# Attention and mixture-of-experts layer on one core: normalizations moved to ScalarE, both halves of the cross projections made by GpSimd

## What is computed

```python
x = layernorm(x + self_attention(x))            # 16 heads of 16, rotary q and k, no bias
x = layernorm(x + cross_attention(x, context))  # q from x; k, v from the context; biases b_q, b_k, b_v, b_o
x = layernorm(x + moe(x))                       # 8 experts, 2 chosen, 2 shared

def layernorm(x):                               # over the 256 features, no gain and no shift
    return (x - mean(x)) / sqrt(var(x) + 1e-5)
# cross attention: qh = q @ w_q.T + b_q, kh = k @ w_k.T + b_k, softmax(qh kh^T / 4) vh, then w_o, b_o
```

## Time and profile before

| | before |
|---|---|
| median of 3 runs | 1545.46 us |
| lowest and highest run | 1537.97 and 1546.08 us |
| the profiled execution, its own time | 1557.11 us |
| its span, first to last instruction | 1555.4 us |
| TensorE busy | 1402.5 us, 90% |
| VectorE busy | 1115.6 us, 72% |
| ScalarE busy | 907.3 us, 58% |
| GpSimd busy | 439.5 us, 28% |
| mean granted TensorE clock | 0.94 of full |

### The profile page before, as it was taken

The page is one execution under the profiler, slowest core; times in us unless marked ns, Lnnn a source line. Parts: engine busy times, 40 slices in busy tenths (PEclk is TensorE's granted clock), DMA queues, the critical chain, the costliest instruction groups (busy, mean ns, idle before and its releaser), DMA issues. The chain is left out here.

```text
span 1555.4 us, 27690 instructions
## 1 busy us (share of the span) xinstructions
PE 1402.5 (90%) x8424; PEld 845.7 (54%) x8424; DVE 1115.6 (72%) x2282; ACT 907.3 (58%) x1702; POOL 439.5 (28%) x411
## 2 busy tenths in 40 slices
PE   2889899999999999999999998999588889999984
PEld 2424354544435444454444443443277779999974
DVE  3788388888789888889879878757256544555466
ACT  3276547656666666666766676646245445555544
POOL 4211131032014013105103201100125544666654
PEclk8699889989999999999999999979789889999997
DMA  3451622433343343244243334140135435778762
GB/s 124 126 159 35 188 81 77 138 103 120 105 136 121 102 128 125 67 148 121 77 139 109 117 101 137 42 110 2 37 136 185 155 105 109 154 131 165 150 178 82
DMA packets 108089, 179.85 MB, mean 116 GB/s; under 512 B 20288, under 2 KB 65984, under 8 KB 103872
## 3 DMA queue, kind: packets, MB, share of 16 engines
q1 hardware_dynamic: 93376, 159.11, 33.1%
q0 software_dynamic: 14592, 19.41, 7.1%
HBM read 98.09 MB, written 79.30 MB: 114 GB/s over the span
## 5 line engine op out<-in xcount | busy, mean ns | idle before, releaser
L618 DVE TENSOR_REDUCE nm<-ps_max 128x1 f32<-128x512 f32 x1024 | 640.6, 681 | 107.0 <-PE ps_max L810 106.7
L576 ACT ACTIVATE prob<-ps_sc 128x512 f32<-128x512 f32 x1024 | 557.9, 597 | 267.5 <-PE ps_sc L824 262.9
L810 PE MATMUL ps_max<-qk 48*128 48x512 f32 x1024 | 442.2, 494 | 31.4 <-DVE nm L618 17.1
L824 PE MATMUL ps_sc<-qk 50*128 50x512 f32 x1024 | 406.6, 466 | 34.0 <-ACT prob L576 33.7
L824 PEld LDWEIGHTS ps_sc<-qk 50*128 50x128 f32 x1024 | 166.5, 189 | 346.5 <-ACT prob L576 294.4
L841 PE MATMUL ps_out<-prob,va 128*32 128x512 f32 x2048 | 279.7, 619 | 1.4 <-ACT prob L576 1.2
L810 PEld LDWEIGHTS ps_max<-qk 48*128 48x128 f32 x1024 | 177.6, 192 | 90.7 <-DVE nm L618 68.7
L1573 PE MATMUL ps_gu<-x2f,we 128*128 128x256 f32 (+1 forms) x1344 | 222.1, 320 | 4.6 <-ACT sg L1238 2.4
L1573 PEld LDWEIGHTS ps_gu<-x2f,we 128*128 128x128 f32 x1344 | 189.2, 191 | 21.9 <-DVE h L1464 3.1
L458 POOL TENSOR_TENSOR rstd<-mv,eps 128x2 f32<-128x2 f32 x32 | 6.4, 201 | 621.7 <-DVE mv L687 621.7
L1573 PE MATMUL ps_dn<-we,hf 128*128 128x256 f32 x864 | 122.6, 298 | 11.3 <-DVE totals L1547 10.5
(11 more groups left out here) (145 smaller groups left out, 1467.3 us busy)
## 6 DMA issues: line engine op xcount, KB each, us to landing
qk<-hbm_self SPq DMA_DIRECT2D x384, 64.0 KB, 2.4
qk<-hbm_cross SPq DMA_DIRECT2D x384, 64.0 KB, 2.3
hbm_self<-stage SPq DMA_DIRECT2D x16, 1024.0 KB, 4.0
hbm_cross<-stage SPq DMA_DIRECT2D x16, 1024.0 KB, 4.2
slots_x<-zeros SPq DMA_DIRECT2D x8, 1360.0 KB, 5.9
xs<-slots_x SPq DMA_DIRECT2D x40, 272.0 KB
weraw<-w_moe SPq DMA_DIRECT2D x11, 768.0 KB
x2in<-x SPq DMA_DIRECT2D x16, 512.0 KB, 4.3
```

Source lines behind the costliest of these rows:

```text
L576: nc.scalar.activation(prob[:, s % 2, j, :], ps_sc[:, (HG * s + j) % NSC, :], ACT.Exp, scale=HD ** -0.5).then_inc(exp_done[a], 1)
L618: nc.vector.tensor_reduce(nm[:, g % 2, r:r + 1], ps_max[:, n % NMX, :], axis=AX.X, op=ALU.max, negate=True).then_inc(max_done[a], 1)
L810: nc.tensor.matmul(ps_max[:, n % NMX, :], qk[rows, 0, pair, P * c:P * c + P], qk[rows, 1, pair, :], start=True, stop=True).then_inc(smax_d ...
L824: nc.tensor.matmul(ps_sc[:, n % NSC, :], qk[rows, 1, h // 2, P * c:P * c + P], qk[rows, 0, h // 2, :], start=True, stop=True).then_inc(st_ ...
```

## The change

The normalizations `ln0` and `ln1` move from VectorE to ScalarE, as an affine step: scale `rstd` and bias `shift` = -mean x `rstd`. GpSimd makes `shift`, by two more small instructions for each `w0` and `w1` half.

For `ck` and `cq`, ScalarE evicts the projection with its bias once, unrounded, into a new buffer `raw_ck` or `raw_cq`, and frees the bank of `ps_job` by that. GpSimd makes both halves from the buffer: the high part by adding a broadcast zero with an fp32r output, then the low part by subtraction. VectorE has no part in either any more. The wait for `self_out` moves from ScalarE to GpSimd, and SyncE's transfers to `hbm_cross` wait for GpSimd's `parts_done` instead of VectorE's count.

```diff
--- before.py
+++ after.py
@@ -90,7 +90,8 @@
 ORDER = [task for half in (FIRST, SECOND) for s in sorted(TASKS[half]) for task in TASKS[half][s]
          if task[0] in PER and task[0] not in ("x", "c")]
 assert len(ORDER) % 2 == 0
-SPLIT = ("q", "k", "ck", "cq", "xt", "nt0", "nt1", "nm0", "nm1", "x", "c")
+SPLIT = ("q", "k", "xt", "nt0", "nt1", "nm0", "nm1", "x", "c")
+KEPT_RAW = ("ck", "cq")
 
 
 def exists(b):
@@ -220,6 +221,9 @@
         res = sb("res", [P, TT, D])
         rot = res[:, :, :].rearrange("p (a u) d -> p a (u d)", a=2)
         cosq = sb("cosq", [P, 2, T])
+        job_raw = {kind: sb(f"raw_{kind}", [P, FC, T]) for kind in ("ck", "cq")}
+        shift = sb("shift1", [P, TT, 1])
+        mone = sb("mone1", [P, TT, 1])
         stage = sb("stage", [P, FC, SLOTS, T], F32R)
         qk = sb("qk", [P, 2, H // 2, T], F32R)
         va = sb("va", [P, 2, TT, H, 2 * HD])
@@ -254,6 +258,7 @@
         read = {k: sem(f"{k}_read") for k in job_done}
         hi_done = {k: sem(f"{k}_hi") for k in SPLIT}
         lo_done = {k: sem(f"{k}_lo") if k in ("q", "k", "x", "c") else read[k] for k in SPLIT}
+        parts_done = {k: sem(f"{k}_parts") for k in KEPT_RAW}
         sin_done = {k: sem(f"{k}_sin") for k in ("q", "k")}
         roped = {k: sem(f"{k}_roped") for k in ("q", "k")}
         self_out = [sem(f"self_out{m}") for m in range(FC)]
@@ -375,14 +380,14 @@
 
                 if h.name == "second" and isinstance(h.k, int) and h.k == -1:
 
-                    sp.wait_ge(consts, 6)
+                    sp.wait_ge(consts, 7)
                     sp.wait_ge(w_hi, 1)
                     sp.wait_ge(w_ready, 1)
                 for s in range(h.steps):
                     if s in h.cross and exists(h.cross[s][0]):
                         b, m = h.cross[s]
-                        sp.wait_ge(lo_done["cq"], upto("cq", b, m))
-                        sp.wait_ge(lo_done["ck"], upto("ck", b, m))
+                        sp.wait_ge(parts_done["cq"], 2 * upto("cq", b, m))
+                        sp.wait_ge(parts_done["ck"], 2 * upto("ck", b, m))
                         sp.dma_start(hbm_cross[m], stage[:, m, :, :].bitcast(F32)).then_inc(cross_out[m], 16)
                     for kind, n, b in h.table.get(s, []):
                         if kind in ("nm0", "nm1"):
@@ -424,17 +429,31 @@
             nc.gpsimd.memset(eps[:, :, :], EPS).then_inc(consts, 1)
             nc.gpsimd.memset(one[:, :], 1.0).then_inc(consts, 1)
             nc.gpsimd.memset(zeros[:, :], 0.0).then_inc(consts, 1)
-            pool.wait_ge(consts, 6)
+            nc.gpsimd.memset(mone[:, :, :], -1.0).then_inc(consts, 1)
+            pool.wait_ge(consts, 7)
             pool.wait_ge(consts_dma, 48)
 
             def split_lo(kind, b, n, out, value, high):
 
                 pool.wait_ge(hi_done[kind], upto(kind, b, n))
                 nc.gpsimd.tensor_tensor(out, value, high.bitcast(F32), ALU.subtract).then_inc(lo_done[kind], 1)
+
+            def both_parts(kind, b, n):
+
+                c = 2 if kind == "ck" else 0
+                pool.wait_ge(self_out[n], (b + 1 if exists(b + 1) else b) * 16 + 16)
+                pool.wait_ge(read[kind], upto(kind, b, n))
+                nc.gpsimd.tensor_tensor(stage[:, n, c + HI, :], job_raw[kind][:, n, :], zeros[:, 0:1].to_broadcast([P, T]), ALU.add) \
+                    .then_inc(parts_done[kind], 1)
+                pool.wait_ge(parts_done[kind], 2 * (b * 2 + n) + 1)
+                nc.gpsimd.tensor_tensor(stage[:, n, c + LO, :], job_raw[kind][:, n, :], stage[:, n, c + HI, :].bitcast(F32),
+                                        ALU.subtract).then_inc(parts_done[kind], 1)
 
             def half(h):
                 for s in range(h.steps):
                     for kind, n, b in h.table.get(s, []):
+                        if kind in KEPT_RAW:
+                            both_parts(kind, b, n)
                         if kind in ("q", "k"):
 
                             c = 0 if kind == "q" else 1
@@ -457,8 +476,13 @@
                             pool.wait_ge(mv_done[a], b * TT + 2 * n + 2)
                             nc.gpsimd.tensor_tensor(rstd[:, at, :], mv[:, at, 1:2], eps[:, at, :], ALU.add) \
                                 .then_inc(var_done[a], 1)
-                            pool.wait_ge(var_done[a], upto(kind, b, n))
+                            nc.gpsimd.tensor_tensor(shift[:, at, :], mv[:, at, 0:1], mone[:, at, :], ALU.mult) \
+                                .then_inc(var_done[a], 1)
+                            pool.wait_ge(var_done[a], 3 * (b * 2 + n) + 1)
                             nc.gpsimd.tensor_tensor(rstd[:, at, :], rstd[:, at, :], mhalf[:, at, :], ALU.pow) \
+                                .then_inc(var_done[a], 1)
+                            pool.wait_ge(var_done[a], 3 * (b * 2 + n) + 3)
+                            nc.gpsimd.tensor_tensor(shift[:, at, :], shift[:, at, :], rstd[:, at, :], ALU.mult) \
                                 .then_inc(rstd_done[a], 1)
                         if kind == "x1b":
                             pool.wait_ge(ln_done[SELF], b * TT + TT)
@@ -525,13 +549,23 @@
                     act.wait_ge(in_sem["c"], b * 16 + 16)
                     wait_done(act, job_done["w0"], "w0", b, 1)
                     split_hi("c", b, 0, cf[:, HI, :, :], raw[:, :, :])
-                if kind == "ck":
-
-                    act.wait_ge(self_out[n], (b + 1 if exists(b + 1) else b) * 16 + 16)
-                    split_hi(kind, b, n, stage[:, n, 2, :], bank(kind, n, b), bcol[:, 1, n:n + 1])
-                if kind == "cq":
-                    act.wait_ge(self_out[n], (b + 1 if exists(b + 1) else b) * 16 + 16)
-                    split_hi(kind, b, n, stage[:, n, 0, :], bank(kind, n, b), bcol[:, 0, n:n + 1])
+                if kind in KEPT_RAW:
+                    act.wait_ge(job_done[kind], upto(kind, b, n))
+                    if exists(b - 1):
+                        act.wait_ge(parts_done[kind], 2 * upto(kind, b - 1, n))
+                    c = 1 if kind == "ck" else 0
+                    nc.scalar.activation(job_raw[kind][:, n, :], bank(kind, n, b), ACT.Identity, bias=bcol[:, c, n:n + 1]) \
+                        .then_inc(read[kind], 1)
+                if kind in ("ln0", "ln1"):
+                    a = int(kind[2])
+                    if a == SELF:
+                        wait_done(act, job_done["xt"], "xt", b - 1, 1)
+                        if exists(b - 1):
+                            act.wait_ge(x1b_done, (b - 1) * TT + TT)
+                    for t in range(TT):
+                        act.wait_ge(rstd_done[a], b * 2 + t // 2 + 1)
+                        nc.scalar.activation((res if a else x1)[:, t, :], res[:, t, :], ACT.Identity,
+                                             scale=rstd[:, t, :], bias=shift[:, t, :]).then_inc(ln_done[a], 1)
                 if kind == "nt1":
                     wait_done(act, job_done["cv"], "cv", b + 1, 1)
                     split_hi(kind, b, n, nf[:, HI, n, :], bank(kind, n, b), bcol[:, 2, n:n + 1])
@@ -634,10 +668,6 @@
                     nc.vector.tensor_tensor(cosq[:, c, :], bank(kind, n, b), trig[:, 0, :], ALU.mult)
                     nc.vector.stream_shuffle(rot[:, c, :], bank(kind, n, b), [p ^ 1 for p in range(32)]) \
                         .then_inc(read[kind], 1)
-                if kind == "ck":
-                    split_lo(kind, b, n, stage[:, n, 3, :], stage[:, n, 2, :], bcol[:, 1, n:n + 1])
-                if kind == "cq":
-                    split_lo(kind, b, n, stage[:, n, 1, :], stage[:, n, 0, :], bcol[:, 0, n:n + 1])
                 if kind == "nt0":
                     split_lo(kind, b, n, nf[:, LO, n, :], nf[:, HI, n, :])
                 if kind == "nt1":
@@ -685,16 +715,6 @@
                     for t in (2 * n, 2 * n + 1):
                         wait_alone(dve, stat_done[a], b * TT + t + 1, w_hi, 1)
                         nc.vector.bn_aggr(mv[:, t, :], st6[:, t, :]).then_inc(mv_done[a], 1)
-                if kind in ("ln0", "ln1"):
-                    a = int(kind[2])
-                    if a == SELF:
-                        wait_done(dve, job_done["xt"], "xt", b - 1, 1)
-                        if exists(b - 1):
-                            dve.wait_ge(x1b_done, (b - 1) * TT + TT)
-                    for t in range(TT):
-                        dve.wait_ge(rstd_done[a], b * 2 + t // 2 + 1)
-                        nc.vector.tensor_scalar((res if a else x1)[:, t, :], res[:, t, :], mv[:, t, 0:1],
-                                                rstd[:, t, :], ALU.subtract, ALU.mult).then_inc(ln_done[a], 1)
 
             def half(h):
                 for s in range(h.steps):
...
```

More of the change, by code:

```diff
@@ L718, in _ @@
             pe.wait_ge(w_ready, 2)
-            pe.wait_ge(consts, 6)
+            pe.wait_ge(consts, 7)
             pe.wait_ge(w_hi, 1)
```

## The result

| | before | after |
|---|---|---|
| median of runs on one chip | 1544.05 us (4 runs, 1537.97 to 1546.08) | 1561.05 us (4 runs, 1556.41 to 1564.41) |
| ratio | | 1.0104, interval 1.0074 to 1.0134 |
| profiled execution | 1557.11 us | 1556.41 us |
| its span, its mean granted clock | 1555.4 us, 0.936 | 1554.7 us, 0.930 |

What follows compares the result with a forecast made beforehand. Bound by the scores-Exp ring, TensorE in projection steps, VectorE only in lumps. 7.4 + 1.9 - 6.0 + 3.8 - 0.8 + 1.4 + 0.75 = +8.5 us on 1545.5 gave 1554.0 us, range 1541 to 1563.

Steps and rivals of the forecast that it cites:

- the likeliest case: Whole kernel: lengthened and shortened steps sum to +8.5 us, 0.55% slower; chance 0.50, of which 0.35 above the bound.
- a rival with 0.13: Behind both closes' stalls: one more low-clock window of 12 us each, +7.2, so +15.7 in all, 1561 us; chance 0.13.
- The case's own range: Whole kernel: the forecast's own range around +8.5 us, +1 to +14.
- ln0 in the passes: Steps around ln0: ScalarE's four normalizations delay Exp, lateness handed on whole, +1.24 us a pass, six times: +7.4 us.
- The walk: Steps 11 to 13 around ln0: third score 1.17 us late, fourth 1.37, next Exp pair 1.25.
- ln1 in the passes: Step of ln1: wait for Exp replaces wait for a maximum, +0.1 us in five passes, +1.4 in the sixth: +1.9.
- ck and cq: Cross projections in the passes: VectorE's relief brings late maxima forward, -1.0 us a pass, six times: -6.0 us.
- The closes: Both closes: cross transfers leave 1.9 us later, +3.8 us; ln0 there ends 0.4 earlier each, -0.8 us.
- The rival that hides them: Closes: late cross projections are hidden there too, +4.7 us in all, 1550 us; chance 0.15.
- The end: ln1 of batch 6 on ScalarE +1.4 us; batch 7 in series, small instructions and last two tiles, +0.75 us.
- my own mark: Loop pass: 126.3 us becomes 126.6; forecast wrong if the pass shrank by a microsecond or more.

Runs made afterwards that it cites:

- cross_passes: Kernel before with only the cross projections of batches 1 to 6 on ScalarE and GpSimd, normalizations on VectorE: 1544.86 us, ratio 1.0000.
- ln_only: Kernel before with only the normalizations moved to ScalarE, cross projections as before: 1564.20 us, ratio 1.0148.
- cross_warm: cross_passes with the third maximum matmul of step 13 of each first half repeated five times: 1553.55 us, ratio 0.9917.
- before_warm: Kernel before with a maximum matmul of step 13 of each first half repeated five times: 1556.46 us, ratio 0.9963.
- before_x1b: Kernel before with only GpSimd's x1b held back until VectorE has done ln1: 1556.08 us, ratio 0.9951.
- cross_only: Kernel before with all cross projections by ScalarE and GpSimd, normalizations on VectorE: 1550.88 us, ratio 1.0042.
- after_again: The changed kernel, unchanged, run again against the kernel before on another chip: 1578.36 us, ratio 1.0105.
- the filling: One maximum matmul issued six times instead of once ahead of the wait behind ln1; changed kernel 1.0040, cross_passes so filled 0.9917, kernel before 0.9963.

## Why the prediction came out as it did, point by point

The direction was right and the time lay in the range. The size was off by a factor of two, and the sum behind it was not what cost the time: the likeliest case gave +8.5 us by its steps, of which some 2 were there; the rest was the clock, which I had as a rival with 0.13. The case's own range, +1 to +14 us, missed the 17; that 1561.05 us lies within 1541 to 1563 is owed to the room left for that rival, and to luck.

**ln0 in the passes, +7.4.** The mechanism was right: TensorE waits for Exp, and the lateness is handed on. The size was 0.75 + 0.17 = 0.92 us a pass, so +5.5. The walk had the third and fourth score 1.17 and 1.37 us late; in the pass shown, against that of the earlier trace rows, they were 0.93 and 1.08. It took the lateness as handed on whole, but the job behind the fourth maximum had stood 0.72 us behind the fourth score and now stands 0.51, and `ln0`'s own step ended only 0.75 us late. The step behind it added the 0.17.

**ln1 in the passes, +1.9.** One wait took the other's place, as forecast. The step became 0.19 us shorter instead of 0.1 longer, and the sixth pass 1.1 us longer for 1.4: together +0.15.

**ck and cq, -6.0.** I read four steps and had -1.0 a pass. The four steps gave -0.86; but the step at the loop's edge gave 0.52 more, four times, which I had not looked at, and the two such steps at the ends of the loop went from 4.46 to 4.23 and from 4.51 to 4.13. In all -7.8. `cross_passes` has -5.9 at equal clock. GpSimd's pair is hidden in the passes, as forecast.

**The closes, +3.8 and -0.8.** The transfer leaves 1.8 us later, for 1.9. What reaches the first maximum is 2.0 us in the first close (21.40 us from the eviction, for 19.36) and 1.2 in the second (14.78 for 13.60), where less of the delay reached it: +3.2. The rival that hides them is refuted. The steps of `ln0` in the closes fell from 5.04 to 4.13 and from 5.02 to 4.27 us, 0.8 each for the forecast 0.4: -1.65.

**The end, +1.4 and +0.75.** The lump of batch 6 costs 1.74 us: `cross_passes`, with the low clock there but VectorE's `ln1`, has 11.67 us for the three steps, and after 13.41. That is the most it can be, as the clock is low in the whole first of these steps in after and only at its end in `cross_passes`; `ln_only`, low for its last microsecond, has 13.11, which gives 1.4. The low clock adds 2.8 us to it, but that is not shown to be the change's: `cross_passes`, `cross_warm`, `before_warm` and `before_x1b`, all with `ln1` on VectorE, have it there too, and only the two profiles of before and `cross_only` don't. For batch 7, from the last statistics to the end of the last normalization it is 2.84 us for 2.32: +0.5.

**The sum.** The undisturbed pass is 125.55 us, where I had said 126.6, and would have been wrong by my own mark had it been 0.25 less. 5.5 + 0.15 - 7.8 + 3.2 - 1.65 + 1.74 + 0.5 = +1.6 us, against +8.5 predicted and +4.3 measured at equal clock. The parts bear it out: the steps give +6.2 for the normalizations, `ln_only` has +6.0 at equal clock; -4.6 for the cross projections, `cross_only` has -3.6.

**The step that failed** is the one by which I priced the clock: "Behind the first close's stall, 12 us had a mean granted clock of 0.70", one such window more behind each close, and against it "the low spell is there already, and 2 us add little". I looked for spells only where TensorE's wait is longest. Most came where it is busy for nine tenths and waits about 1 us once in a pass, up to 4 us a time. The trace of before had one in the passes, 3.7 us in the first overlapping pass, and I read other passes and did not see it. In the second close the rival was right in kind: behind the stall the clock is low for 24 us without a break in both profiles of after, for 3 and 10 us with a gap between in both of before. That stage is 3.3 us longer in `after`, though the later transfer brings only 1.2 and `ln0` gives back 0.75; some 3 us are the clock. The rival's sum (+15.7) is near the measured 17, for the greater part by a wrong place.

**What stays open.** Why a spell comes in one pass and not in the next. `cross_passes` has the same `ln1` as before with about the same wait, and had a spell in five passes of five where before had one; the matmuls of the filling did not prevent all of them. TensorE's busy time in the five microseconds of `ln1` does not order the cases: 3.91 us in before, where the clock held, and 4.10 us in `cross_passes`, where it fell right behind. A rival that no run tests is that the moment at which the wait falls decides, and not only its length; a kernel before with a short delay ahead of the passes would tell. What is shown is where the time goes, and that the spells behind `ln1` go in the first five passes when its wait and the load beside it go. The count of spells from one profile each is thin; the mean clock of all runs says the same, 0.9180 for `after_again` against 0.9331.

## What to carry to other kernels

In a kernel whose TensorE is busy for nine tenths, read the granted clock of each pass in windows before pricing an edit: a wait of about 1 us that already costs one spell in six passes can cost five after an edit that leaves the steps no longer, and a mean over passes hides it. Walk a moved lump through its own step, as that was right within 0.5 us each time, and look at every step in which the relieved engine has work, the loop's edge too. And before moving VectorE's work elsewhere, see what GpSimd does beside it: one wait that kept the two apart took 1.35 us off a step and, with the cross projections of the passes on GpSimd, gave 1.6 and 1.5% less than before on two chips, where the change as made gave 1% more.

## What the runs showed of the hardware that I had not expected

- The clock falls to the 1.2 GHz level for about 7 or 10 us at a time behind a wait of TensorE of about 1 us, in some passes of the same code and not in others; one of 10 us costs 3.7 to 4.0 us here, one of 7 us 2.2 to 2.5. Between kernels of nearly the same work it makes up 15 us of 1550.
- A relief of VectorE that shortens steps by 1.4 us a pass can give nothing at all (`cross_passes`, 1.0000), since the mean clock went from 0.9397 to 0.9338.
- GpSimd's add of 128x512 with a one-column broadcast operand takes 1.04 us, less than the 1.28 us with two whole operands.
- The kernel before differs by 20.7 us between two chips (1544.62 and 1565.29 us), more than the change itself makes. In the profiles the stretch behind the last value product differs, 435 to 443 us on the first and 454 to 460 us on the second.
